# A graph network of four layers: POOL starts a group of gathers when the rows of the group before it have landed

## The reference

```python
h = maximum(layernorm(x), 0);  x = x + segment_sum((h * W0)[src], dst)
h = maximum(layernorm(x), 0);  x = x + sage(relu(sage(h)))       # two mean aggregations over the edges, linear layers
h = maximum(layernorm(x), 0);  x = x + relu(edge_softmax(edge_attr, dst) weighted sum of (h @ W_fc.T)[src] + eh, + h @ loop_W)
h = maximum(layernorm(x), 0);  x = x + segment_sum((h @ W3.T + b3)[dst], src) / degree
```

## Time and profile before

| | us |
|---|---|
| median of 3 runs | 12801.77 |
| lowest, highest | 12754.38, 12835.04 |
| the profiled execution, its own time | 12898.33 |
| its span, first to last instruction | 12895.1 |
| granted TensorE clock, mean | 0.592 |
| POOL busy, 8,320 gathers | 8182.5 |
| PE busy | 4042.5 |
| DVE busy | 3867.4 |
| ACT busy | 472.8 |

### The profile page before, as it was taken

How to read it: one execution, slowest core, us unless ns; L and a number is a source line. 1 busy time by engine, 2 the same in 40 slices (tenths; PEclk the granted TensorE clock), 3 DMA queues, 4 the chain that set the end, 5 groups by cost and what they waited for, 6 DMA issues and landing times.

```text
span 12895.1 us, 84333 instructions
## 1 busy us (share of the span) xinstructions
PE 4042.5 (31%) x18630; PEld 3047.8 (24%) x18631; DVE 3867.4 (30%) x4123; ACT 472.8 (4%) x740; POOL 8187.2 (63%) x8343
## 2 busy tenths in 40 slices
PE   1332333243343344222222224444444432222222
PEld 1111111122222222111111113433343321111111
DVE  3323323333333333344344312222222221111111
ACT  0000000011111111000000000000000000000000
POOL 4666666666666666677667665555565556666666
PEclk7565556566666666555555556676676665555555
DMA  4333333344344444213333212222222221111111
GB/s 91 99 96 92 98 92 98 90 133 120 114 129 129 122 131 122 60 34 56 56 55 62 43 40 62 62 62 60 61 64 63 61 44 37 36 36 36 36 36 35
DMA packets 712143, 951.29 MB, mean 74 GB/s; under 512 B 289361, under 2 KB 504401, under 8 KB 709597
## 3 DMA queue, kind: packets, MB, share of 16 engines
q0 software_dynamic: 266240, 385.62, 14.7%
q10 hardware_dynamic: 208528, 441.95, 11.4%
q1 hardware_dynamic: 237075, 120.64, 3.2%
HBM read 737.19 MB, written 206.15 MB: 73 GB/s over the span
## 4 chain that ended last, share of the span: by engine, by line
another core or an unknown queue 36%; issue 28%; PE 12%; POOL 9%; DVE 8%; DVEq 3%; ACT 2%; ACTq 1%; DMA 1%; SPq 0%; POOLq 0%
POOL flat L282 9%; PE pair L1068 5%; PE pair L918 3%; DVE flat L418 2%; PE wide L932 1%; PE flip L989 1%; DVEq L214 1%; PE flip L990 1%; DVE flat L680 1%; DVEq L418 1%; ACT flat L814 1%; DVE flat L522 1%; ACT flat L810 1%; DVE flat L575 1%
## 5 line engine op out<-in xcount | busy, mean ns | idle before, releaser
L282 POOL DMA_INDIRECT flat<-table,stage x8320 | 8182.5, 983 | 4687.4 <-issue 2447.4
L918 PE MATMUL pair<-flat 128*128 x9760 | 1582.9, 338 | 5305.8 <-issue 3750.8
L918 PEld LDWEIGHTS pair<-flat 128*128 x9760 | 1185.0, 132 | 5767.1 <-issue 5700.5
L1068 PE MATMUL pair<-flat 128*128 x4880 | 1190.7, 412 | 1535.4 <-DVE flat L680 1234.5
L418 DVE TENSOR_TENSOR flat<-fixed,dcol 128x1024 f32 x915 | 1076.9, 1218 | 1901.3 <-remote 1133.8
L1068 PEld LDWEIGHTS pair<-flat 128*128 128x128 f32 x4880 | 1076.7, 248 | 1649.5 <-issue 1648.3
L680 DVE TENSOR_TENSOR flat<-fixed,dcol 128x512 f32<-128x512 f32 x610 | 417.4, 690 | 1809.7 <-remote 1298.7
L460 DVE TENSOR_REDUCE batch<-pair 128x65 f32<-128x195 f32 (+1 forms) x392 | 139.4, 356 | 2627.9 <-remote 1524.2
L932 PE MATMUL wide<-flat,wbd 128*128 128x512 f32 x840 | 594.7, 860 | 351.6 <-DMA flat<-gate_d 137.3
L989 PE MATMUL flip<-ident,flat 128*128 128x128 f32 x840 | 352.5, 422 | 989.7 <-ACT flat L814 480.0
L418 DVE TENSOR_TENSOR flat<-fixed,flat 128x1024 f32 x305 | 362.1, 1220 | 931.5 <-remote 589.6
(11 more groups left out here) (142 smaller groups left out, 1811.6 us busy)
## 6 DMA issues: line engine op xcount, KB each, us to landing
flat<-table,stage POOLq DMA_INDIRECT x8320
flat<-in_ea ACTq DMA_DIRECT2D x140, 768.0 KB
ex_d<-flat ACTq DMA_DIRECT2D x140, 768.0 KB
flat<-ex_d SPq DMA_DIRECT2D x208, 512.0 KB
flat<-gate_d ACTq DMA_DIRECT2D x280, 192.0 KB
pm_d<-flat ACTq DMA_DIRECT2D x70, 768.0 KB
flat<-pm_d ACTq DMA_DIRECT2D x70, 768.0 KB
sort_d<-flat ACTq DMA_DIRECT2D x14, 1024.0 KB
```

The source lines that it names most:

```text
L282: pool.indirect_dma_start(out=to_row, out_offset=None, in_=tables[p], in_offset=bass.IndirectOffsetOnAxis(ap=stage[:, st, c:c + 1].bitcast ...
L918: mm = M(bank[a % 2][:, 0:width], flat[:, ds(at_one[k], P * 2)].bitcast(bf16), flat[:, ds(at_row[k], TW * 2)].bitcast(bf16)[:, 0:width], s ...
L1068: mm = M(bank[a % 2][:, 0:F3], ohf[:, k, :], exr[:, ds(g % XR, 1), k, :].rearrange("p o c -> p (o c)"), start=first and k == 0, stop=False)
```

## The change

Ahead of each group but the first of a pass, POOL waits also for the semaphore `landed` of the group before it, to the same count for which SP waits at L330: all eight gathers of group `g - 1` have landed. The wait stands ahead of the one for `slots_free`. Nothing else changes; the ring keeps its four slots.

```diff
@@ -274,6 +274,9 @@
                     slot, st = g % SLOTS, g // SG % 2
                     if g % SG == 0:
                         pool.wait_ge(staged[st], 16 * (p * (G // SG // 2) + g // SG // 2 + 1))
+                    if g >= 1:
+
+                        pool.wait_ge(rows_at[(g - 1) % SLOTS], CH * 16 * (G // SLOTS * (p % 3) + (g - 1) // SLOTS + 1))
                     if g >= SLOTS:
                         pool.wait_ge(s["slots_free"], g - SLOTS + 1)
                     for k in range(CH):
```

## The result

| | before | after |
|---|---|---|
| median, us | 12805.31 | 13026.27 |
| lowest, highest | 12754.38, 12835.04 | 13017.85, 13049.63 |
| ratio after / before | | 1.0176 (95%: 1.0149 to 1.0204) |
| span of the profiled execution | 12895.1 | 13019.5 |

The account below looks back on a forecast made before the run. No engine is full; five gather passes set the pace, with POOL stopping for slots behind a backlog. Passes 12361 + 483 = 12844 us, 194 more than now; profiled 13092, median 12993 us, 1.5% slower; whole range 12420 to 13800.

Parts of the forecast that it names:

- the backlog: POOL's gather stream demands about 11.1 us a group, is issued in 10.0; PE's signals sit behind what builds up.
- the 160 stops without a releaser: POOL's waits for ring slots with no releaser found, 758.3 us: all expected to be replaced by the new wait.
- The pause: Gap at each group boundary on POOL: 1.7 us in place of 0.30, so 11.4 us a group, not 10.0.
- The 77 with PE's matmul as releaser are true lateness of the consumers: POOL's slot waits on PE's matmul, 613.7 us: each gives 1.7 us to the new gap, 483 us stay.
- Late landings: Rows arriving late beside ACT's large blocks, first three passes: 200 us added, half of 416; ends 0 and 416.
- slow gathers: Slower gathers in the second and third pass and elsewhere: 171 + 105 + 30 us added to the passes.
- The fourth pass: 98 POOL waits for DVE's product, 646.8 us, expected gone: pass at the new pace, 0 to 350 us more.
- What would show it: Signs if right: POOL's usual gap 1.7 us; third and fifth pass 2370 to 2520 us, second above 2650, fourth under 2600.
- Steadier pauses free the consumers: Rival, chance 0.29: a pause in each group lets PE's signals through, the 483 us go; median 12320 to 12515 us.
- Short pauses free nothing: Rival, chance 0.22: every POOL stop stays and the landing adds 980 us at 700 boundaries; median 13774 to 13975 us.
- The estimate by the page's figure: Skill page's 2.0 us DMA cost, uncovered at 1035 boundaries: 1760 us more, 14,660 us profiled; not used in the forecast.
- the factor 0.9925: Ratio of median to profiled execution before (12801.77 / 12898.33), used to turn 13092 us profiled into a 12993 us median.

Follow-up runs that it names:

- the last run: Kernel before, no landing wait; POOL makes two fills of 904 elements in each group, `hidT` shares the memory of `hT`: 12464.88 us, ratio 0.9722.

## Why the prediction was right, and where it was not

The sign, the size and the main mechanism (the backlog) held, and two terms of the sum were wrong in opposite directions.

- *The bound.* That the 160 stops without a releaser were a backlog of the stream, not lateness of PE, held in every run: they go with the pace, whether the wait is on a landing or on a fill, and neither more slots nor the wait alone moves them. The value of 11.1 us a group comes from four stops in the earlier trace rows, of which the fourth, 6.80 us after four groups, does not fit the rule that the prediction draws from them (5.8). Over more stops the rule is rough: in the fifth pass before, stops without a releaser after four groups last from 0.9 to 5.9 us and those after five from 1.9 to 7.4. The limit in the runs lies a little higher than 11.1: at 11.14 and 11.16 us a group 44 and 51 stops without a releaser are left, at 11.45 none.
- *The pause.* Forecast 1.7 us and 11.4 us a group; measured 1.83 and 11.52. The restart of POOL behind the landing was the mis-sized part, 0.2 us in place of 0.1. The two together are worth 1,035 x 0.13 = 135 us more than forecast.
- *"The 77 with PE's matmul as releaser are true lateness of the consumers", 483 us.* This step failed. None of it stayed: with the slower pace these waits vanish as well, in the second pass too. The longest of them in the trace before, 27.0 us, shows what it was made of. The timelines of PE, DVE and POOL, second pass:

```profile
4856.91 0.37 PE L943 MATMUL pair<-zb 128*128 128x192 bf16 x1
```

```profile
4878.63 0.36 DVE L460 TENSOR_REDUCE batch<-pair 128x64 f32<-128x192 f32 x1 [31.52 <-remote]
```

```profile
4911.81 4.04 POOL L282 DMA_INDIRECT flat<-table,stage  x1 [26.95 <-PE pair L918]
```

  The matmul ends at 4857.28 and DVE takes up its sum 21 us later. Only then does the dense work of seven tiles begin, and only after it does DVE build the one-hots for which PE's next visit waits. That visit frees the slot, so the profile names the right releaser, but 21 us of its lateness came from the late signal; by an estimate from these rows some 6 us of the 27.0 were the engines' own work. A plain name in the releaser's column is no proof that the engine was late by its own work. For the other 76 waits this is inferred from their end at the slower pace.
- *Late landings, 200 us taken, 0 to 416 given.* This failed as well, and upwards. The five passes take 12798.5 us; less 1,040 x 9.70 for the issue, 325 for slow gathers (8204.06 busy less 8,320 x 0.947) and 1,035 x 1.83 for the usual gap, some 490 us are left, the same that the comparison with the last run gives. The halving was wrong, and so was its reason, that one block delays several groups in a row. Counted as late when SP's signal comes over 2.4 us after the last gather's end, the second pass of the trace before has 53 late groups, and only 9 times is the next group late too. In the changed kernel the landings themselves moved: late groups went from 51 to 35 in the first pass, from 53 to 81 in the second and from 19 to 15 in the third. By what they last over 1.6 us, the first pass came near the half that was taken (91 us, of 166 at full weight), the third near full weight (70 of 83), and the second far above it (266 us, against 166). Why the second pass has more of them was not tested.
- *The fourth pass.* Taken at the new pace; it came at 2436 us, 65 above 208 x 11.4. Its gain of 286 us is the largest change of any pass. The reason given for it held: SP's waits for PE's signals ahead of the edge values shrank from 1942.8 us to 521.5 (446.2 with PE as releaser, 75.3 without one).
- *What would show it.* The fourth under 2600, the second above 2650 and the fifth in 2370 to 2520 came as written; the third, 2587 us, came above that range, by the late landings and the slower pace.
- *The rivals.* "Steadier pauses free the consumers" was right in its mechanism: a pause of 1.8 us in each group is enough, and all stops go. It was wrong in its price because the same wait lays the late landings open. With a pause that does not, the kernel takes 12465 us, inside the 12320 to 12515 that this rival gave. "Short pauses free nothing" was refuted. The rule of the Trainium skill (DMA: Bandwidth & Descriptors, Rules for kernel authors), to issue a DMA early and wait late, agrees with the sign that the runs show, and in the fourth pass, which gained 286 us by waiting at once, the trace goes against it. The estimate by the page's figure, 14,660 us profiled, is far from the span of 13019.5 us, since the pauses took the place of the stops.

So 483 us too much and some 444 too little (135, 290 and 19 of slow gathers) nearly cancel: the passes were put at 12844 us and take 12798.5. That the median lies 33 us above the forecast all the same comes of the factor 0.9925 from the profiled execution to the median, 99 us, less 24 us by which the time outside the passes came out shorter. The changed kernel's profiled execution, 13022.64 us, is as long as its median, 13026.27. The good agreement of the total is in part luck.

## What to carry to other kernels

When an engine waits with no releaser, or for an instruction that by its record ended long before, compare the length of the waits with the length of the stream of gathers ahead of them; if they grow together, slow the stream before adding buffers. Slow it by something that costs a fixed time and depends on nothing (here two short fills on POOL in a group: 2.8% faster than before), not by a wait for the landing, which also takes over every late landing of the busy passes (1.8% slower). A wait for the landing pays where the stops that it removes cost more than the slower pace and the late landings, as in the fourth pass alone (2.1% faster). Few late landings are not enough: the fifth pass has hardly any, and its 16 us are no more than two executions differ by.

## What the runs showed of the hardware that I had not expected

- While POOL streams gathers of 128 rows, one in 1.25 us, what PE has finished can show up late for the others, for DVE by up to 34.1 us. The signals of SP and DVE are prompt where the trace before lets one see it: PE starts 0.57 us after SP's signal (median of the 63 waits that the profile puts down to it) and, in the fourth pass, 0.21 us after DVE's one-hots (median of 178). After the last gather of such a stream it takes about 1.4 us plus 1.1 us for each group of eight, a fit to four stops that holds roughly for the others and for one of 15.24 us after twelve groups. At one gather in 1.43 us (11.45 us a group) the lateness no longer holds anybody. What resource the gathers and PE's signals share is open: no run varied the rows' size or the number of packets.
- The limit is nearly the same for rows of 256 bytes (fourth pass) and of 392 bytes (first and fifth): both are free of stops at 11.45 us. At 11.16 us with one undivided pause the fourth pass still has 40 waits for the product, 234.8 us; with two half pauses, and the fill behind the wait for the slot, it has 16, 74.5 us.
- TensorE's granted clock, which stands at 0.5 (1.2 GHz) or 1 (2.4 GHz) and is given here as the mean over the fourth pass, rose from 0.68 to 0.72 where the stops of that pass were nearly gone (the changed kernel, the wait in the fourth pass alone, the last run). PE did the same matmuls there in a shorter time, with shorter waits between them.
- A ring of eight slots in place of four changed no pass by more than 30 us, which is within what two executions differ by.
